# Reordering ScalarE's and VectorE's work around GELU in two steps of a fused attention and slot-router kernel

## The reference

```
x = x + local_attention(ctx, layernorm(x))     # 34 context rows per batch, Gaussian weights, tanh(cat @ Wc.T)
x = x + slot_router(layernorm(x))
# slot_router: h = gelu(x @ w1 + b1); logits = (h @ w2 + b2) / tau'; top 8 of 64, softmax -> alpha
#   slots = alpha.T @ x / sum(alpha); GRU gates; attention among slots; layernorm; out = alpha @ (slots @ W)
```

## Time and profile before

| what | value |
|---|---|
| median of 3 runs | 343.57 us (343.3 to 344.89) |
| the profiled execution's own time | 343.45 us |
| its span in the trace | 341.6 us |
| busy share PE, VectorE, ScalarE, GpSimd | 96%, 73%, 59%, 60% |
| mean granted TensorE clock | 0.991 |

### The profile page before, as it was taken

The page is one execution under the profiler, slowest core; times in us unless marked ns, Lnnn a source line. Parts: engine busy times, 40 slices in busy tenths (PEclk is TensorE's granted clock), DMA queues, the critical chain, the costliest instruction groups (busy, mean ns, idle before and its releaser), DMA issues.

```text
span 341.6 us, 7115 instructions
## 1 busy us (share of the span) xinstructions
PE 327.2 (96%) x2316; PEld 282.8 (83%) x2316; DVE 250.0 (73%) x751; ACT 201.8 (59%) x408; POOL 205.9 (60%) x350
## 2 busy tenths in 40 slices
PE   8999999999999999999999999989999999999970
PEld 6688768998998989989989989977789877777750
DVE  5799887766785877877877777757935674678872
ACT  3485264659569578776778678576753355223430
POOL 5001459787877886785776767636683337046772
PEclk9999999999999999999999999999999999999996
DMA  7999967423242332322423100019600000000897
GB/s 279 310 321 384 326 175 216 121 67 123 63 122 66 91 97 64 123 64 63 124 64 97 59 2 2 0 16 356 225 3 0 2 0 0 0 2 1 340 368 277
DMA packets 40950, 42.79 MB, mean 125 GB/s; under 512 B 3261, under 2 KB 32061, under 8 KB 40914
## 3 DMA queue, kind: packets, MB, share of 16 engines
q1 hardware_dynamic: 38960, 40.19, 36.0%
q10 hardware_dynamic: 1666, 1.49, 1.4%
q0 software_dynamic: 288, 0.66, 0.7%
HBM read 32.18 MB, written 8.39 MB: 119 GB/s over the span
## 4 chain that ended last, share of the span: by engine, by line
PE 75%; POOL 9%; issue 7%; ACT 5%; DVE 2%; POOLq 0%; ACTq 0%; DVEq 0%
PE psum L465 17%; PE psum L466 16%; PE psum L467 16%; PE psum L1775 4%; PE psum L2040 3%; POOL hT_lo L610 3%; PE psum L1806 3%; PE psum L1604 2%; PE psum L1755 2%; PE psum L1843 2%; ACT th L1335 1%; POOL r2all L621 1%; PE psum L1577 1%; PE psum L1664 1%; PE psum L1989 1%
## 5 line engine op out<-in xcount | busy, mean ns | idle before, releaser
L465 PE MATMUL psum<-GW_hi,hT_hi 128*128 128x292 f32 (+1 forms) x256 | 78.7, 307 | 0.1
L467 PE MATMUL psum<-GW_lo,hT_hi 128*128 128x292 f32 (+1 forms) x256 | 73.9, 289 | 0.0
L466 PE MATMUL psum<-GW_hi,hT_lo 128*128 128x292 f32 (+1 forms) x256 | 73.9, 289 | 0.0
L615 POOL TENSOR_TENSOR X<-X,th 128x512 f32<-128x512 f32 x32 | 38.7, 1210 | 28.1 <-ACT th L1335 28.1
L465 PEld LDWEIGHTS psum<-GW_hi,hT_hi 128*128 128x128 f32 x256 | 48.4, 189 | 1.5 <-issue 1.1
L466 PEld LDWEIGHTS psum<-GW_hi,hT_lo 128*128 128x128 f32 x256 | 48.3, 189 | 0.1
L467 PEld LDWEIGHTS psum<-GW_lo,hT_hi 128*128 128x128 f32 x256 | 48.1, 188 | 0.0
L982 DVE BATCH_NORM_STATS2 st<-X 128x6 f32<-128x512 f32 x32 | 22.2, 693 | 25.2 <-POOL X L615 25.2
L610 POOL TENSOR_TENSOR hT_lo<-xT,hT_hi 128x512 fp32r<-128x512 f32 x30 | 39.2, 1306 | 2.0 <-DVE stack L993 2.0
L465 PE MATMUL psum<-xhT_hi,w_hi 128*128 128x256 f32 x128 | 37.8, 296 | 0.8 <-issue 0.5
L466 PE MATMUL psum<-xhT_hi,w_lo 128*128 128x256 f32 x128 | 36.1, 282 | 0.0
(11 more groups left out here) (319 smaller groups left out, 905.4 us busy)
## 6 DMA issues: line engine op xcount, KB each, us to landing
xT<-in_xT SPq DMA_DIRECT2D x32, 256.0 KB, 2.7
X<-in_x SPq DMA_DIRECT2D x32, 256.0 KB, 3.5
out<-ost SPq DMA_DIRECT2D x32, 256.0 KB, 3.0
WhhT<-in_WhhT SPq DMA_DIRECT2D x1, 3072.0 KB, 13.6
WihT<-in_WihT SPq DMA_DIRECT2D x4, 768.0 KB, 8.0
Wo<-in_wo ACTq DMA_DIRECT2D x4, 256.0 KB, 4.4
WvpT<-in_WvpT SPq DMA_DIRECT2D x4, 256.0 KB, 5.1
WaT<-in_WaT SPq DMA_DIRECT2D x1, 1024.0 KB, 11.4
```

What stands on the lines that cost most here:

```text
L465: pe.matmul(out, w_hi, m_hi, start=start, stop=False)
L466: pe.matmul(out, w_lo, m_hi, start=False, stop=False)
L467: return pe.matmul(out, w_hi, m_lo, start=False, stop=stop)
L615: pool.tensor_tensor(tile_x(r), tile_x(r), halves(th[:, :]), ALU.add).then_inc(S("x2"), 1)
```

## The change

Four things are moved, in two pairs of steps, 7 with 8 and 11 with 12 (`GELU_HELD`):

1. `high_xh(5)` and `high_xh(9)` go from the start of steps 8 and 12 to the end of steps 7 and 11, ahead of GELU.
2. The second half of GELU goes from the end of steps 7 and 11 into steps 8 and 12, behind `turned_weights`.
3. `norm2(6)` and `norm2(10)` go ahead of `exp_of(8)` and `exp_of(12)`.
4. On VectorE `low_xh(5)` and `low_xh(9)` stand ahead of `stats2(6)` and `stats2(10)`, not behind them.

No instruction is added or taken away. The order of ScalarE around steps 7 and 8 is

```diff
+GELU_HELD = (7, 11)
...
         def step(s):
             if live(s - 3):
                 low_xh(s - 3)
+            if s - 1 in GELU_HELD:
+                stats2(s - 2)
...
-            if live(s - 1) and s < NT - 1:
+            if live(s - 1) and s < NT - 1 and s not in GELU_HELD:
                 stats2(s - 1)
...
         def step(s):
             if s in TOPK_STEP:
                 logits_biased(TOPK_STEP.index(s))
-            if live(s - 3):
+            if live(s - 3) and s - 1 not in GELU_HELD:
                 high_xh(s - 3)
             if live(s - 1):
                 turned_weights(s - 1)
+            if s - 1 in GELU_HELD:
+                gelu(GELU_STEP.index(s - 1), 1)
+            if s - 1 in GELU_HELD:
+                norm2(s - 2)
             if live(s):
                 exp_of(s)
-            if live(s - 2):
+            if live(s - 2) and s - 1 not in GELU_HELD:
                 norm2(s - 2)
...
+            if s in GELU_HELD:
+                high_xh(s - 2)
             if s in GELU_STEP:
                 gelu(GELU_STEP.index(s), 0)
-                if s < NT - 1:
+                if s < NT - 1 and s not in GELU_HELD:
                     gelu(GELU_STEP.index(s), 1)
```

## The result

| | median of 21 runs | lowest to highest |
|---|---|---|
| before | 343.3 us | 342.27 to 345.05 |
| after | 345.0 us | 344.23 to 345.83 |

The ratio is 1.0047 with a 95% interval of 1.0038 to 1.0056, so the kernel is 1.3 to 1.9 us slower.

A forecast was written before the change was run, and what follows sets the result against it. PE, busy 96%, sets the pace from 106 us, the loop through the tanh before; PE's savings are given back and the late tanh leaves 1.47 us, so 343.45 and 1.5, plus 0.12, give 345.0 us; range 343.3 to 346.0.

The forecast's parts named there:

- What bounds the kernel: Main loop: waits run on PE alone from 106.02 us; before that the loop is as slow as PE.
- ScalarE, steps 7/8: High copy waits for nothing; norm2(6) waits 0.47 us for nm; tanh of tile 7 ends at 86.25, 0.59 late.
- VectorE: Step 8: low_xh(5) ahead of stats2(6) costs nothing, and the first layer's 0.36 us wait goes.
- Where the gain goes: Start of step 9: PE's 1.05 us gain is all given back waiting for tanh_of(7), and 0.06 more.
- The sum: Whole kernel: 343.45 us of the profiled execution and 1.5 make 344.95; with 0.12 for the median, 345.0 us.
- 0.16 us of room: PE at score(14): gap between tanh_of(12)'s end at 114.92 and score's start at 115.08 before, read as slack.
- the room swallows it: Lower bound on the late tanh's spread: room of 0.16 to 0.5 us in the loop absorbs it.
- The gain is kept: Rival, both places: 1.1 and 1.0 us come off, 341.5 us, if tanh_of(7) ends before 85.14; chance 0.05.
- About even: Rival: ScalarE does not wait at norm2, so the tanh stays where it was; 343.6 us; chance 0.27.
- More than that: Rival: high_xh(9) ahead of GELU waits for late PE, or later GELU steps stall PE; 346.1 us; chance 0.18.
- The rule weighed: ScalarE table loads: the skill states about 1283 ns plus a 1380 ns drain; the rows show only the first.

The follow-up runs named there:

- e7: Kernel before with only high_xh ahead of an undivided GELU and low_xh ahead of stats2, norm2 behind exp; ratio 0.9997, 343.14 us.
- e1: Changed kernel with the third move undone: norm2(6) and norm2(10) behind exp again; ratio 0.9988, 343.44 us.
- e2: Kernel before with the third move alone: norm2(6) and norm2(10) ahead of exp; ratio 1.0034, 344.98 us.
- e4: Changed kernel with tanh_of(7) and tanh_of(11) directly behind GELU's second half, ahead of norm2; ratio 1.0024, 344.48 us.
- e3: Kernel before with the whole change in steps 11/12 only; ratio 1.0026, 344.33 us.
- e5: e4 plus stats2(7), stats2(11) ahead of the softmax weights and scales2(7), scales2(11) ahead of low_x; ratio 0.9949, 341.80 us.
- e6: e5 with VectorE's row offsets, and the scaling of Wp that follows, one step later; ratio 0.9953, 341.76 us.
- e8: e5 without GpSimd's move of scales2 ahead of low_x; ratio 0.9981, 343.31 us.

## Why the prediction was right, and where it was off

- **What bounds the kernel.** Right in the main. Up to tile 13 PE can't get ahead of the loop, and from there on PE carries whatever it has: the table's last two columns differ by 0.03 us at most, and e7 shows the limit with nothing else changed. The boundary was put too early. The chain of waits runs on PE alone from 106.02, the start of `context` of tile 11, but what PE has in hand there is not kept: in e1 it is 0.64 us, at tile 12 0.32, and at tile 13 nothing.
- **ScalarE, steps 7/8.** Right: the high copy starts without a wait at 79.61 (forecast 78.95 + 0.67 = 79.62), the wait for `nm` is 0.46 us (0.47), the tanh is 0.58 late (0.59). In steps 11/12 the wait is 0.82 (about 0.9) and the loop +1.57 (1.58).
- **VectorE.** Right that the low part ahead of the statistics costs nothing and ends the first layer's wait (e7). The size was a little off: the first layer follows the context by 0.34 us after and in e7, not by 0.25.
- **Where the gain goes.** Right: two waits for `th`, 2.3 us together. e2 shows that the late tanh alone makes the whole of the loss.
- **The sum.** 1.5 forecast, 1.6 measured (1.3 to 1.9). The term that was small is the step from the tanh's end to PE's matmul: I took 0.05 us, which is what PE's `context` needs behind `aTs`, and behind `th` it is 87.06 - (86.25 + 0.67) = 0.14. With it the shift at the end of the loop is 1.55 and not 1.47. The same term explains the "0.16 us of room" that I read at `score(14)` before (and that `score(10)` shows too): 0.14 us of it is this step, so PE stood at the tanh there already and hardly any room was left. The bound "the room swallows it" had no more than 0.02 us to rest on at that place. That the forecast meets 345.0 to the tenth is in part luck: before has a median of 343.3 over 21 runs where I built on 343.57, and the loss is larger than forecast by about as much.
- **Rivals.** "The gain is kept" failed at the point that was named, the tanh's end. "About even" is e1 and not the change. "More than that" did not happen: the high copy ahead of GELU starts 0.50 us behind `hT_hi` at the first place, on time, and 0.57 at the second, which is 0.06 late by my 0.51, and later GELU steps add nothing (+1.55 at tile 30).
- **The rule weighed.** The table load starts 0.03 us behind the copy's end (79.61 + 0.58 = 80.19, 80.22) and takes 1.28, as before. In every run each load starts 0.01 to 0.03 us behind the instruction ahead of it; no drain of 1.4 us appears in any run, and with one the wait of 0.46 would not have been there.
- **Not foreseen.** The late exp pushes the softmax weights' last instruction into GpSimd's residual. In the changed kernel it takes 1.12 us (87.12 to 88.24), but PE turns the weights at 88.74 only, so it costs nothing there. As soon as the tanh was mended, it was what ended last (e4), for PE and for the statistics behind it, and the expectation of e4 failed on it.

That GpSimd's `nm` is 0.4 us later in the second place is in the timeline of before, and e3 shows what it costs. What makes it so was only read off that timeline and not tried:

```profile
101.44 0.42 DVE L1014 SCALAR_TENSOR_TENSOR kept<-kept,lsub 128x256 f32<-128x256 f32 x1
101.50 0.45 POOL L604 TENSOR_SCALAR ve<-mr 128x2 f32<-128x2 f32 x1
...
102.75 0.42 DVE L1022 TENSOR_TENSOR A<-kept,kr 128x256 f32<-128x256 f32 x1
102.84 0.40 POOL L606 TENSOR_TENSOR sd<-ve,rr 128x2 f32<-128x2 f32 x1
```

The two GpSimd instructions take 0.23 and 0.19 us in step 7. Here each starts behind an instruction of VectorE's top-8 work and ends 0.07 to 0.09 us behind it. The 0.43 us that they take longer are the whole of the difference.

## What to carry to other kernels

Where an engine is packed, a new order can't make its last instruction earlier unless that instruction is moved itself; ask for each instruction that is moved forward whether its input is there, since its wait goes to all that is queued behind it. A stall of the busiest engine is worth only the room that the loop around it leaves in the next turn, so first move what closes the loop (here the tanh, then statistics and scales) and only then mend the stall. A move that loses can gain together with another: the changed kernel with the early tanh was 0.2% slower than the kernel before, and with the loop's next links moved too it was 0.5% faster.

## What the runs showed of the hardware

- A VectorE instruction of 0.26 us (128x36, two inputs in SBUF) takes 1.12 to 1.16 us in steps 8 and 12 when it starts behind a GpSimd instruction of 1.19 to 1.29 us, and ends 0.04 to 0.06 us behind it; beside small GpSimd instructions it stays at 0.26 (e5). No trace here has one that started inside such a GpSimd instruction and stayed short. The low part with one input in PSUM ran beside the same GpSimd work in its usual 0.66 to 0.69 us. It goes the other way too: a GpSimd instruction of 0.22 us (`ve`) that starts behind VectorE's row offset takes 0.54 to 0.71 and ends 0.07 to 0.08 us behind it (after, e4, e6, e8). The Trainium skill (SBUF — State Buffer, Who interferes with whom) states that a VectorE instruction with two SBUF inputs contends with a GpSimd instruction that reads SBUF, because its second input comes through the read interface that they share. The trace agrees. In e8 PE waited 1.4 us for it in the two places together.
- PE's first matmul starts 0.14 us behind the end of the tanh that it waits for (87.06 behind 86.92 after), and 0.05 us behind the end of the copy `aTs` (82.62 behind 82.57 before).
- Tanh runs behind GELU without a table load of its own: in e4, e5 and e8 it starts 0.72 us after the second pair of GELU instructions began, and the next load stands ahead of exp. That is what made the early tanh cheap.
